# Making sixteen instead of eighteen depthwise rows per band, the two others through a small DRAM tensor, with another order of work between the two layers

## The reference

```python
# layer 0: per 8x8 window
q, k, v = conv1x1(x, Wq, bq), conv1x1(x, Wk, bk), conv1x1(x, Wv, bv)     # then cut into windows
attn = softmax(einsum('bgck,bgcl->bgkl', q, k) / sqrt(128))
x = x + einsum('bgkl,bgcl->bgck', attn, v)
x = x + conv1x1(gelu(conv1x1(x, W1, b1)), W2, b2)
# layer 1
enh  = dw3x3(conv1x1(x, w_conv1_pw, b_conv1_pw), w_conv1_dw, b_conv1_dw)       # pad 1
h    = grouped3x3(x, w_conv2_g, b_conv2_g)                                     # 16 channels, pad 1
h1, h2 = split(h)
attn = conv1x1(h1 * h2, w_conv2_pw, b_conv2_pw) * attgamma + conv1x1(x, w_conv211, b_conv211)   # 16 channels
attk = einsum('bpn,nm->bpm', attn, selfw)      # 128*2*9 weights for each pixel p
y    = einsum('bpgij,bpgj->bpgi', attk, patches3x3(enh)) + einsum('bpn,nc->bpc', attn, selfb)
out  = y * ga1 + enh + x
```

## Time and profile before

| | us |
|---|---|
| median of 3 executions (5592.13 to 5592.62) | 5592.44 |
| the profiled execution | 5592.69 |
| its span, from the first to the last instruction | 5591.0 |
| layer 0: up to the barrier | about 1870 |
| from there to the first product of layer 1 (DVE) | about 52 |
| 64 bands | about 3669 |

### The profile page before, as it was taken

The page is one execution under the profiler, slowest core; times in us unless marked ns, Lnnn a source line. Parts: engine busy times, 40 slices in busy tenths (PEclk is TensorE's granted clock), DMA queues, the critical chain, the costliest instruction groups (busy, mean ns, idle before and its releaser), DMA issues.

```text
span 5591.0 us, 112546 instructions
## 1 busy us (share of the span) xinstructions
PE 5429.2 (97%) x37896; PEld 3904.3 (70%) x37896; DVE 5155.3 (92%) x5413; ACT 3471.9 (62%) x4284; POOL 4484.5 (80%) x1959
## 2 busy tenths in 40 slices
PE   8999999999999699999999999999999999999998
PEld 7888888888887366666666666666666666666666
DVE  7888888888888499999999999999999999999999
ACT  6888888888887455555555555555555555555553
POOL 4555555666555699999999999999999999999996
PEclk9999999999999799999999999999999999999999
DMA  2222222222221122222222222222222222222221
GB/s 89 75 75 75 75 75 75 71 72 75 75 75 64 56 71 73 65 77 62 69 73 68 72 69 74 64 77 63 69 73 68 72 68 75 63 77 64 68 74 44
DMA packets 155248, 394.18 MB, mean 71 GB/s; under 512 B 35137, under 2 KB 38401, under 8 KB 155137
## 3 DMA queue, kind: packets, MB, share of 16 engines
q1 hardware_dynamic: 155200, 393.56, 22.6%
HBM read 219.37 MB, written 136.31 MB: 64 GB/s over the span
## 4 chain that ended last, share of the span: by engine, by line
PE 45%; DVE 16%; issue 4%; DVEq 1%; POOL 0%; SPq 0%; ACT 0%; DMA 0%; POOLq 0%
PE ps_k L981 18%; PE ps_t L998 12%; DVE products L1165 11%; PE ps_m L964 8%; DVE products L1171 3%; PE ps_p L951 3%; PE ps_t L1006 2%; PE ps_t L1015 1%; DVE ps_k L1165 1%; PE ps_t L1013 1%; DVE h_prod L1185 1%; POOL enh L917 0%; DVEq L119 0%; SPq L870 0%; DVEq L1169 0%
## 5 line engine op out<-in xcount | busy, mean ns | idle before, releaser
L917 POOL TENSOR_TENSOR enh<-enh,tap 128x1280 f32<-128x1280 f32 (+1 forms) x1024 | 2514.5, 2456 | 224.8 <-ACT tap L1114 178.5
L1165 DVE TENSOR_TENSOR products<-ps_k,enh 128x1024 f32<-128x1024 f32 x1664 | 2001.0, 1218 | 76.2 <-PE ps_k L981 50.0
L981 PE MATMUL ps_k<-att,basis 128*128 128x512 f32 x4608 | 1730.4, 461 | 88.6 <-DVE products L1171 43.6
L981 PEld LDWEIGHTS ps_k<-att,basis 128*128 128x128 f32 x4608 | 719.7, 189 | 870.9 <-DVE products L1165 528.1
L476 POOL TENSOR_TENSOR hidden_lo<-hidden,hidden_hi 128x1024 fp32r<-128x1024 f32 x256 | 694.9, 2735 | 730.2 <-DVE hidden_hi L687 730.2
L1114 ACT ACTIVATE tap<-e,dw 128x1280 f32<-128x1280 f32 (+1 forms) x1024 | 1253.4, 1249 | 4.4 <-POOL enh L917 4.4
L923 POOL TENSOR_TENSOR products<-products 128x1024 f32<-128x1024 f32 x384 | 920.1, 2396 | 74.3 <-DVE products L1165 74.3
L1165 DVE TENSOR_TENSOR ps_k<-ps_k,enh 128x1024 f32<-128x1024 f32 x640 | 784.0, 1225 | 31.8 <-PE ps_k L981 30.8
L1171 DVE TENSOR_TENSOR products<-ps_k,products 128x1024 f32<-128x1024 f32 x640 | 783.5, 1224 | 22.0
L998 PE MATMUL ps_t<-ident_swap,products 128*128 128x128 f32 x5120 | 768.6, 273 | 0.0
L998 PE MATMUL ps_t<-ident,products 128*128 128x128 f32 x5120 | 766.9, 272 | 0.0
(11 more groups left out here) (117 smaller groups left out, 7360.3 us busy)
## 6 DMA issues: line engine op xcount, KB each, us to landing
xin<-layer_out SPq DMA_DIRECT2D x64, 1280.0 KB, 7.2
xt<-in_x SPq DMA_DIRECT2D x128, 512.0 KB, 4.0
layer_out<-xo SPq DMA_DIRECT2D x128, 512.0 KB, 2.9
x_own<-layer_out SPq DMA_DIRECT2D x128, 512.0 KB, 3.8
out<-out_sb SPq DMA_DIRECT2D x256, 256.0 KB, 2.0
att<-att_hi SPq DMA_DIRECT2D x512, 32.0 KB, 2.0
att<-att_lo SPq DMA_DIRECT2D x512, 32.0 KB, 2.0
h_up<-h_sb SPq DMA_DIRECT2D x256, 16.0 KB
```

What stands on the lines that cost most here:

```text
L917: nc.gpsimd.tensor_tensor(own, own, tap_sb[add % TAP_BUFFERS][:, 0:hi - lo, :], ALU.add).then_inc(dw_done, 1)
L981: mm = nc.tensor.matmul(ps_k[KERNEL_BUFFER[q]][:, BANK * s:BANK * (s + 1)], basis[:, 2 * t + s, :], att[p][:, j, :], start=True, stop=True)
L1165: nc.vector.tensor_tensor(out, kernels, enh[p][:, r:r + CHUNK_ROWS, dx:dx + W].unsqueeze(1).to_broadcast([C, 2, CHUNK_ROWS, W]), ALU.mult) ...
```

## The change

For a band it makes rows 2 to 18 of enh and takes rows 0 and 1 from the band above, whose rows 16 and 17 they are:

- HALVES begins at row 2, so each of the first eight taps covers eight rows and not ten, on ACT and POOL.
- The pointwise chunks begin at row 2 of xin: four of four rows and a last one of two rows. ACT has one instruction for each chunk, and there is no bias_top.
- There is a DRAM tensor edge_rows, with nine slots for an image. When a band n is complete, SP writes its rows 16 and 17 there (`keep_edge`, after enh_ready) and, when that has landed, reads them back into rows 0 and 1 of the next band (`fetch_edge`). Both stand ahead of `move_h2` on SP. `clear_outside` for the top row is gone; enh_ready counts one a band.
- The first band of each image needs a row of its own: row 1 is the image's first row of enh. For all eight images at once, PE makes the pointwise rows (`top_rows`, four matmuls), ACT adds the bias (`bias_top_rows`), DVE makes the six taps that lie inside the image (`make_top_rows`, two groups of six instructions), and SP writes them into slot 0 (`keep_top_rows`), all ahead of the first product.
- The transition is in another order. pwT, `make_columns`, `make_grouped`, `make_basis` and `split_basis` move from layer 0 to the start of `convolve`, and `load_pointwise` moves to step 1 of layer 0. The first band's whole grouped convolution follows its pointwise chunks; `h_rows` and `att_high` of that band come between its first taps on ACT, and `coefficients` at once on PE.

PE, from the barrier to the first rows of the second band's grouped convolution, before. ring and ps_ are PSUM tiles; a name in brackets is the semaphore it waits for.

The diff, cut to its core:

```diff
-HALVES = ((0, 10), (10, 18))
+HALVES = ((2, 10), (10, 18))
...
-                prepared.load_pointwise(sp)
...
                     if isinstance(l, int) and l == 1:
+                        prepared.load_pointwise(sp)
                         prepared.load_shared(sp)
...
-                pe.wait_ge(wt_ready, 6)
-                pe.wait_ge(prepared.loaded["pointwise"], 16 * prepared.LOADS["pointwise"])
-                nc.tensor.matmul(ring[1][:, 0:C], prepared.pw_raw[:, :], ident[:, :], is_transpose=True,
-                                 start=True, stop=True).then_inc(wt_done, 1)
-                pe.wait_ge(wt_ready, 8)
+                pe.wait_ge(wt_ready, 7)
                 pe.wait_ge(w_lo_ready, 1)
...
-                    if isinstance(l, int) and l == 6:
-                        prepared.make_columns(dve)
-                    if isinstance(l, int) and l == 7:
-                        prepared.make_grouped(dve)
-                    if l is None and m is not None:
-                        prepared.make_basis(dve)
-                    if l is None and m is None and n is not None:
-                        prepared.split_basis(dve)
...
+                sp.dma_start(x_top[:, :, :], x2[:, :, PAD:PAD + 2, :].rearrange("b c h w -> c b (h w)")).then_inc(x_top_in, 16)
+
+                def keep_top_rows():
+                    sp.wait_ge(top_step, (TAPS - 3) * len(top_groups))
+                    sp.dma_start(edge_rows[:, 0, :, :].rearrange("b c w -> c b w"), top.rearrange("c b h w -> c b (h w)")).then_inc(top_written, 16)
+                    sp.wait_ge(top_written, 16)
+
+                def keep_edge(n, p):
+                    sp.wait_ge(enh_ready, n + 1)
+                    sp.dma_start(edge_slot(n, 1), enh[p][:, ROWS:ROWS + 2, :].rearrange("c h w -> c (h w)")).then_inc(edge_written, 16)
+
+                def fetch_edge(m, p):
+                    at_least(sp, edge_written, 16 * m)
+                    sp.dma_start(enh[p][:, 0:2, :].rearrange("c h w -> c (h w)"), edge_slot(m, 0)).then_inc(edge_in, 16)
...
+                    if n is not None and not (isinstance(n, int) and n == bands - 1):
+                        keep_edge(n, p)
+                    if m is not None and not (isinstance(m, int) and m == 0):
+                        fetch_edge(m, b)
                     if m is not None:
                         move_h2(m)
                     if n is not None:
                         store(n, 0)
                     if m is not None:
                         attention_rows(m, b)
+                    if isinstance(m, int) and m == 0:
+                        keep_top_rows()
+                        fetch_edge(m, b)
...
+                nc.gpsimd.memset(top, 0.0).then_inc(edges_ready, 1)
...
+                pe.wait_ge(prepared.loaded["pointwise"], 16 * prepared.LOADS["pointwise"])
+                pe.wait_ge(prepared.ident_ready, 1)
+                nc.tensor.matmul(ps_m[:, 0:C], prepared.pw_raw[:, :], ident[:, :], is_transpose=True,
+                                 start=True, stop=True).then_inc(prepared.pwT_done, 1)
+                pe.wait_ge(prepared.pwT_ready, 1)
                 pe.wait_ge(swap_ready, 2)
-                pe.wait_ge(grouped_ready, 1)
...
+                    elif c > first_banks.index(first_banks[c]):
+                        pe.wait_ge(e0_ready, first_banks.index(first_banks[c]) + 1)
+                    lo, hi = PAD + CHUNK_ROWS * c, min(PAD + CHUNK_ROWS * (c + 1), XROWS)
+                    nc.tensor.matmul((first_banks[c] if first else ps_p)[:, 0:W * (hi - lo)], pwT[:, :], xin[p][:, lo:hi, 1:W + 1],
                                      start=True, stop=True).then_inc(pw_done, 1)
+
+                def top_rows():
+                    pe.wait_ge(x_top_in, 16)
+                    for g, (lo, hi) in enumerate(top_groups):
+                        for first in range(lo, hi, 2):
+                            last = min(first + 2, hi)
+                            mm = nc.tensor.matmul(ps_k[g][:, 2 * W * (first - lo):2 * W * (last - lo)], pwT[:, :], x_top[:, first:last, :],
+                                                  start=True, stop=True)
+                        mm.then_inc(top_done, 1)
...
+                            pe.wait_ge(grouped_ready, 1)
...
+                        pe.wait_ge(top_step, (TAPS - 3) * len(top_groups))
...
+                        group_taps(l, p, 0, TAPS * CHUNKS)
+                        top_rows()
+                        return
+                    first = isinstance(m, int) and m == 0
+                    if first:
+                        coefficients(m)
...
-                        a = nc.scalar.activation(e0[p][:, CHUNK_ROWS * c + lo:CHUNK_ROWS * c + hi, 1:W + 1], ps[:, lo:hi, :],
-                                                 ACT.Identity, bias=bias)
-                    a.then_inc(e0_ready, 1)
+                    lo, hi = PAD + CHUNK_ROWS * c, min(PAD + CHUNK_ROWS * (c + 1), XROWS)
+                    ps = (first_banks[c] if isinstance(m, int) and m == 0 else ps_p)[:, 0:W * (hi - lo)]
+                    nc.scalar.activation(e0[p][:, lo:hi, 1:W + 1], ps.rearrange("c (h w) -> c h w", w=W), ACT.Identity,
+                                         bias=bias_bottom[:, bass.ds(m, 1)] if c == PW_CHUNKS - 1 else bias_pw[:, 0:1]).then_inc(e0_ready, 1)
+
+                def bias_top_rows():
+                    for g, (lo, hi) in enumerate(top_groups):
+                        act.wait_ge(top_done, g + 1)
+                        ps = ps_k[g][:, 0:2 * W * (hi - lo)]
+                        nc.scalar.activation(ps, ps, ACT.Identity, bias=bias_pw[:, 0:1]).then_inc(top_biased, 1)
...
                                 action(items[k], *args)
                             else:
                                 action(items[k], (p + k) % 2, *args)
+                            if first and k == 1 and action is tap_product and args == (0, 5):
+                                h_rows(items[1])
+                            if first and k == 1 and action is tap_product and args == (0, 6):
+                                att_high(items[1], (p + 1) % 2)
+                                bias_top_rows()
...
+                dve.wait_ge(prepared.pwT_done, 1)
+                nc.vector.tensor_copy(pwT[:, :], ps_m[:, 0:C]).then_inc(prepared.pwT_ready, 1)
+                prepared.make_columns(dve)
+                prepared.make_grouped(dve)
+                prepared.make_basis(dve)
+                prepared.split_basis(dve)
                 for p in range(2):
                     nc.vector.memset(att[p][:, :, :].bitcast(FP32), 1.0)
+
+                def make_top_rows():
+                    dve.wait_ge(edges_ready, 2)
+                    step = 0
+                    for g, (lo, hi) in enumerate(top_groups):
+                        dve.wait_ge(top_biased, g + 1)
+                        rows = ps_k[g][:, 0:2 * W * (hi - lo)].rearrange("c (b h w) -> c b h w", h=2, w=W)
+                        for t in (4, 7, 3, 6, 5, 8):
+                            dy, dx = divmod(t, 3)
+                            first, last = max(0, 1 - dx), min(W, W + 1 - dx)
+                            own = top[:, lo:hi, 1, 1 + first:1 + last]
+                            near = rows[:, :, dy - 1, first + dx - 1:last + dx - 1]
+                            if t == 4:
+                                nc.vector.tensor_scalar(own, near, dw[:, t:t + 1], bias_dw[:, 0:1], ALU.mult, ALU.add).then_inc(top_step, 1)
+                            else:
+                                dve.wait_ge(top_step, step)
...
+                    if q == 0:
+                        dve.wait_ge(dw_done, (TAPS - 1) * (2 * n + 1))
+                        dve.wait_ge(edge_in, 16 * n + 16)
+                    if q == 2 * TAPS:
+                        dve.wait_ge(dw_done, (TAPS - 1) * (2 * n + 2))
+                        dve.wait_ge(enh_ready, n + 1)
```

74 lines of the change are left out of this document (38 added, 36 removed).

## The result

The changed kernel takes **5571.12 us** (median of 6 runs, 5568.58 to 5573.64) and the kernel before 5592.53 us (6 runs, 5591.57 to 5592.96): ratio 0.9962, 95% interval 0.9951 to 0.9973. Timed again beside the experiments it was 5569.03 against 5592.35, ratio 0.9959 (0.9945 to 0.9972). It is faster by 21 to 23 us; 5572.5 was forecast.

A forecast was written before the change was run, and what follows sets the result against it. No single engine bounds the kernel; in a band the chain of waits runs along DVE's queue, then PE's. Terms 2.2 + 1.5 + 11.0 + 5.5 = 20.2 off 5592.69 gave 5572.5 us, range 5556 to 5583.

The forecast's parts named there:

- In a band, nothing: In the bands, work spared on POOL, ACT and PE ends no wait of PE or DVE: 0 us.
- Rival 1: The bands get shorter: 0.1 us a band gives 5566, the full 0.5 us 5541; chance 0.12.
- SP back in time: On SP in a band, the edge rows' write and read fit ahead of move_h2, with 4.5 us cover: no cost.
- rival 4: SP returns late between keep_edge and move_h2, delaying h_prod in 62 bands: 5628 at a 7.3 us landing; chance 0.04.
- Start of layer 0: At the start of layer 0, PE no longer waits for the pointwise weights: -2.2 us, bounds 0 and 2.25.
- Steps 6 and 7: In layer 0, DVE's make_columns and grouped preparation instructions leave these steps: -1.5 us, between 0 and 2.3.
- Last steps: At layer 0's end, make_basis and split_basis no longer hold hidden_hi, for which PE waited: -11.0 us, bounds 7 and 12.5.
- Rival 3: The layer 0 gain doesn't arrive whole, since POOL's hidden_lo is next: 5 us of 11, 5578.5; chance 0.07.
- The transition: Between layer 0 and the bands, first product 6.6 us sooner, less 1.1 for POOL: -5.5 us, bounds -9 and 0.
- The write: Ahead of the first product, SP's 1.06 MB of top rows to DRAM take 5.1 us to land.
- The collision of split_basis with POOL's adds: In the transition, one POOL add of 2.2 us falls between DVE's two splits, so h_prod starts at 1894.0.
- POOL's merges: In the first band, POOL's 17 adds and first merge end at 1929.0, wanted at 1927.9: +1.1 us.

The follow-up runs named there:

- e1: The changed kernel with make_columns, make_grouped, make_basis and split_basis back on DVE in layer 0: 5579.79 us.
- e9: The changed kernel with first-band rows by DMA inside SBUF, earlier first merges on POOL, closer second-band chunks on ACT, and three fills on ACT: 5564.51 us.
- e6: The changed kernel once more, unedited: 5569.03 us.
- e10: The changed kernel with one extra 532 KB transfer issued by SP ahead of each keep_edge: 5569.09 us.
- e2: The changed kernel with the spared work of POOL's adds and PE's half pointwise chunk put back as idle work: 5575.73 us.
- e5: The changed kernel with the first band's two upper rows going from top into enh by one DMA inside SBUF: 5569.12 us.

## Why the prediction was right, and where it wasn't

**The whole: right, by 1.4 us** (5571.1 against 5572.5), and within the range. The sum was 20.2 and came out as 21 to 24. By the means two terms were too small, the last steps by 1.6 us and the bands (forecast 0, about 1.2, for a reason that stays open), and the three others 0.2 to 0.4 too large, so part of the errors cancelled.

**In a band, nothing: right.** 57.20 against 57.18 us; with the work put back 57.16 and with less of it 57.165. Rival 1 (shorter bands) is out: even its smallest case, 0.1 us, is more than any run shows. POOL's idle time grew by 4.0 us a band and bought nothing there.

**SP back in time: right.** Forecast cover 4.5 us, measured 5.4. The threshold of rival 4 was put at a landing of 1.95 + 4.5 = 6.4 us; by the measured cover it is 7.3.

**Start of layer 0: right** (-2.2 forecast; the first projection comes 2.11 us sooner, and the cast to x_hi near 45 us comes 2.0 us sooner by the means; the -2.8 of the first pair of profiles is scatter). I counted PE's wait and its matmul. What passed them on was DVE's copy of pwT, which stood in its queue ahead of the splitting of the weights, in the kernel before:

```profile
13.93 0.29 DVE L677 COPY pwT<-ring 128x128 f32<-128x128 f32 x1 [1.95 <-PE ring L498]
14.14 0.62 DVE L679 CAST w_hi<-wT 128x896 fp32r<-128x896 f32 x1
```

w_hi is now at 12.03, 2.11 us sooner.

**Steps 6 and 7: right** (-1.2 of -1.5).

**Last steps: mechanism right, size too small** (-11.0 forecast, -12.6 by the means, just over the bound of 12.5). The stops shrank by 6.24 + 5.17 = 11.4 us, which is what was forecast. The two steps got shorter by 12.7 us (35.34 to 22.62 between the same tiles). I had set the upper bound at PE's two stops. Behind a stop of 6 us, however, PE also runs slowly for a time, as in these windows of the kernel before:

```profile
1819.00:1826.00 7.00, 5.41 (x16) 3.86 (x16) 3.93 (x5) 1.22 (x2) 5.50 (x2) 0.57 0.01 2
1838.00:1846.00 8.00, 6.42 (x18) 4.40 (x20) 1.14 (x3) 1.63 (x2) 4.92 (x2) 0.53 0.00 0
```

A matmul over 512 columns took 0.80 and 0.63 us there and takes 0.51 and 0.39 in the same place now. From 1790 to the start of layer 1 the granted clock was 0.84 of 82.5 us and is 0.90 of 65.3 (0.82 and 0.89 in the second profiles, and 0.83 in e1, where the stops are back), so about half of the stretch at the lower level is gone with the stops. That this makes up the 1.3 us beyond them fits, but no run separates it. Rival 3 (the gain doesn't arrive whole) is out.

**The transition: right as a whole, with the first product too early** (5.5 forecast and 5.1 measured at the second band's first product; at the first product 6.6 forecast and 50.2 - 45.1 = 5.1 by the means, 4.15 in the first pair). Taken from the start of layer 1, in the first profile:

| mark | forecast | measured |
|---|---|---|
| pointwise chunks begin | 1.5 | 3.0 |
| h_prod | 21.5 | 22.9 |
| att_hi | 24.5 | 25.5 |
| last top row | 35.6 | 36.6 |
| the 1.06 MB have landed | 40.7 | 43.5 |
| first product | 43.2 | 45.65 |

The gain itself comes, as the trace has it, from the convolution ahead of the second band's chunks: h_sb begins 17.1 us behind the start of layer 1 where it began 24.6. No run puts the old order back.

One step failed in every profile, the start. I had given DVE's copy of pwT and ident_swap 0.7 us, and bias_bottom and ident_swap together 0.4 of DVE's queue. bias_bottom and ident_swap were over 2.8 us behind the barrier in place of 1.4, since POOL was filling `top`; I hadn't thought of a fill as a thing that could hold DVE, and e9 shows that it does. The write is no such step: 5.1 us was forecast from x_own behind xin, the first profile has 6.9, and the five have 5.0 to 6.9. What makes it vary is open. Where it was quick (e6, e10), the first product waited for PE instead, whose queue the forecast had not looked at: there stand the second band's chunks, which wait for ACT. The collision of split_basis with POOL's adds cost DVE 1.9 us (7.32 where it took 5.40 alone; with the idle 0.49 us ahead of the fill, which the forecast left out, 2.4), against the 2.3 of one add. POOL's two adds beside it took 3.77 and 4.44 us in place of 2.18, so POOL lost 3.9. DVE's queue without the start is right within 0.2 in sum, so the miss at h_prod is the start. The moves of h_up would have let h_prod start at about 22.0 (h_sb ends at 17.76, and 4.25 later), so a shorter queue of DVE alone would win 0.9 us; in e9 the chunks began 1.6 us sooner as well, and h_prod came 1.7 us sooner.

The rule of the Trainium skill, page SBUF — State Buffer, section Who interferes with whom, stood in the prediction with 3 us less if every preparation instruction that could meet POOL is held once. The trace agrees: split_basis with its two inputs in SBUF was held by POOL's adds. It also shows that POOL need not read for this: its fill only writes, and it held a tensor_scalar and a copy (1.95 and 1.87 us against 0.25 and 0.29 without POOL's fill). Beyond the one collision in my sum it cost 1.4 us, all of it in the place that I had not looked at, and not 3.

**POOL's merges: +1.1 forecast; right, though the first profile shows 0.** They were due at 1929.0 and wanted at 1927.9 by my count. In the first profile the merge was done 0.08 us ahead of the sum, since the first product itself came 2.5 us later than forecast and POOL's queue, with its first merge done 57.7 us behind the start of layer 1 where 56.5 was forecast, only 1.2. In the four other profiles of the unedited transition a sum waited for POOL, 2.32, 2.54, 1.33 and 0.87 us. The reading "POOL is next" held: the longer adds of e2 made the wait 3.29 us. With it fits that the second band begins at the same distance whether the first product comes at 43.7 or at 46.1.

## What to carry to other kernels

Work that is spared pays only where its engine is waited for: 260 us of POOL and 170 us of ACT were saved here and nothing of it arrived in 63 bands, while some 4 us of it were worth 5 to 6 us in the first band, where POOL was in debt (e2). Moving preparation out of a stage in which an engine stands still for it into one where it lies beside other work took out the whole stop here, and more (13.5 us), and cost 4 to 5 us at the new place (e1); ask there what else meets it, down to a memset on another engine. When one wait on a path is removed (e5), list the next two before counting the gain: PE's order and POOL's debt stood 1 and 2 us behind, and only with other orders on POOL and ACT and the fills moved (e9) were 4.5 us more won. And before a step of a sum is called right or wrong by 1 or 2 us, profile the same kernel again: three readings of this forecast (the start of layer 0, the write, the merges) look otherwise in a second profile.

## What the runs showed of the hardware

- A memset of 2080 elements on POOL (1.83 us) held two DVE instructions without any common data until it was over: 1.95 and 1.87 us against 0.25 and 0.29 with the fill on ACT, and 0.43 and 0.35 where they were issued ahead of it (e2).
- ACT fills 128x2048 fp32 from one broadcast column in 1.9 us, about as fast as DVE's memset (1.76); the instructions of gT on DVE beside it took 1.33 us, as long as without it.
- DVE's tensor_tensor with two inputs in SBUF beside a chain of POOL's adds: one of two took 4.61 us in place of 2.69, and two of POOL's adds 3.77 and 4.44 in place of 2.18.
- A write of 1.06 MB from SBUF to DRAM, one transfer of one kernel, landed after 5.0 to 6.9 us in five profiles with that part of the kernel unedited.
- PE's granted clock fell for 3.4 us in the last band in one profile of a kernel and not in the other of the same kernel (0.54 against 1.00), which is 1.2 us of that execution; ahead of the first product parts of the transition stood at the lower level in every profile (pairs of matmuls of 2.04 to 2.08 us against 1.02).
- Extra transfers of 520 KB on the same queue delayed a small one behind them by only 0.8 and 1.7 us (one and two of them; landings of 1.9, 2.7, 3.6 us), and by 2.2 for five (4.1); with five, it was SP's issue time, 4.14 us for the five, that grew most.
